# Expert rows in blocks of 256 and of 128 on one Trainium2 core, and another order of the work between the layers

## The reference, cut to what matters

```python
# layer 0: each token goes to its best expert alone
top1 = argmax(x @ gate_W + gate_b)
h = gelu(x[top1 == e] @ W1[e] + b1[e])          # 128 -> 512
out[top1 == e] = h @ W2[e] + b2[e]              # 512 -> 128
x = x + attention0(xn) * silu(out)
# layer 1: each token goes to its two best experts, each of which keeps at most C = 2048 rows
xe[idx1, pos1], xe[idx2, pos2] = x, x           # rows in order of arrival
h = gelu(xe[e] @ W1[e] + b1[e]);  ye = h @ W2[e] + b2[e]
out = w1 * keep1 * ye[idx1, pos1] + w2 * keep2 * ye[idx2, pos2]
x = x + attention1(xn) * silu(out)
```

## Time and profile before

| | us |
|---|---|
| median of 3 runs (lowest, highest) | 1130.6 (1126.27, 1135.07) |
| the profiled execution, its own time | 1132.19 |
| span of its profile | 1130.3 |
| PE busy in the span | 1004.9 (89%) |
| mean granted TensorE clock | 0.951 of full speed |

### The profile page before, as it was taken

One profiled execution on the slowest core, in us unless ns is written; L12 is line 12 of the kernel. 1 busy time (PEld: TensorE's weight loads), 2 busy tenths in 40 slices (PEclk: granted clock), 3 DMA queues, 4 the chain that ended last, 5 costly groups with the idle time before them and its releaser, 6 DMA issues.

```text
span 1130.3 us, 22358 instructions
## 1 busy us (share of the span) xinstructions
PE 1004.9 (89%) x6636; PEld 736.4 (65%) x6636; DVE 686.6 (61%) x2541; ACT 655.2 (58%) x1967; POOL 673.2 (60%) x825
## 2 busy tenths in 40 slices
PE   6688899999999999899999998998889979999940
PEld 2465566666668986566666665666568758989940
DVE  6847776776753346776786777868654443445326
ACT  4329767667754557667666766675554434454534
POOL 5534588888754555676675687887354423545533
PEclk9759899999999999999999999999999889999985
DMA  9200202202526742303302212132130044777755
GB/s 300 58 6 1 43 25 61 65 25 66 160 47 209 221 129 63 74 6 70 65 7 60 54 36 61 34 67 53 40 86 19 29 144 144 214 216 217 214 139 142
DMA packets 97385, 103.70 MB, mean 92 GB/s; under 512 B 10447, under 2 KB 85238, under 8 KB 97040
## 3 DMA queue, kind: packets, MB, share of 16 engines
q1 hardware_dynamic: 90256, 89.96, 30.5%
q0 software_dynamic: 7040, 12.66, 3.3%
HBM read 77.29 MB, written 25.28 MB: 91 GB/s over the span
## 4 chain that ended last, share of the span: by engine, by line
PE 62%; DVE 17%; ACT 7%; issue 6%; POOL 4%; DMA 1%; another core or an unknown queue 1%; SPq 0%; POOLq 0%; DVEq 0%; ACTq 0%
PE bank L1135 11%; PE bank L644 9%; PE bank L633 9%; PE bank L1164 7%; PE bank L1191 5%; PE bank L1179 4%; PE bank L1216 4%; DVE arena L1760 4%; PE bank L1154 3%; ACT arena L1494 3%; DVE arena L1769 2%; POOL arena L910 2%; PE bank L1365 2%; PE bank L1349 1%; ACT arena L1483 1%
## 5 line engine op out<-in xcount | busy, mean ns | idle before, releaser
L1494 ACT ACTIVATE arena<-arena 128x128 f32<-128x128 f32 (+1 forms) x512 | 226.9, 446 | 114.6 <-DVE arena L1760 114.0
L1760 DVE CUSTOM_DVE_ANT_0 arena<-bank,arena 128x128 f32<-128x128 f32 (+1 forms) x512 | 183.0, 413 | 140.8 <-PE bank L1164 133.1
L1135 PE MATMUL bank<-arena 128*128 128x512 f32 x384 | 215.6, 649 | 13.0 <-ACT arena L1483 10.0
L910 POOL TENSOR_TENSOR arena<-arena 128x512 f32<-128x512 f32 x128 | 133.5, 1046 | 146.6 <-ACT arena L1470 141.7
L1769 DVE COPY arena<-bank 128x384 f32<-128x384 f32 x256 | 130.2, 549 | 24.5 <-PE bank L1179 21.4
L607 POOL DMA_INDIRECT expert_out<-arena x78 | 77.0, 988 | 100.8 <-DVE arena L713 85.1
L1470 ACT ACTIVATE arena<-bank 128x512 f32<-128x512 f32 x192 | 112.4, 586 | 31.1 <-PE bank L1135 30.9
L925 POOL TENSOR_TENSOR arena<-arena 128x512 f32<-128x512 f32 x128 | 129.5, 1045 | 1.3
L1164 PE MATMUL bank<-arena 64*128 64x128 f32 (+1 forms) x1024 | 120.8, 355 | 9.6 <-DVE arena L1760 8.9
L1179 PEld LDWEIGHTS bank<-const,arena 128*128 128x128 f32 x768 | 91.9, 142 | 56.8 <-issue 56.6
L1191 PE MATMUL bank<-arena 128*64 128x256 f32 (+1 forms) x1024 | 112.3, 340 | 7.3 <-DVE arena L1769 3.7
(11 more groups left out here) (273 smaller groups left out, 1740.5 us busy)
## 6 DMA issues: line engine op xcount, KB each, us to landing
arena<-in_wp SPq DMA_DIRECT2D x39, 514.0 KB
arena<-recip_rows SPq DMA_DIRECT2D x30, 512.0 KB
XN<-in_wp SPq DMA_DIRECT2D x23, 514.0 KB
arena<-expert_rows SPq DMA_DIRECT2D x62, 129.0 KB
arena<-expert_out SPq DMA_DIRECT2D x16, 256.0 KB, 5.0
arena<-in_b SPq DMA_DIRECT2D x62, 64.0 KB
expert_out<-fill SPq DMA_DIRECT2D x11, 338.6 KB, 8.2
expert_rows<-fill SPq DMA_DIRECT2D x1, 2967.0 KB, 22.0
```

The lines of the kernel that those rows point to most:

```text
L910: pool.tensor_tensor(sq[:, i % 2], r, r, ALU.mult).then_inc(S["sq_done"], 1)
L1135: mm = pe.matmul(RING[bnk][:, :], xa[:, p, t * P:(t + 1) * P], wqkv[:, 512 * k:512 * k + 512], start=True, stop=True)
L1494: ins = act.activation(w, w, ACT.Exp, bias=nm[:, p, 16 * t + h:16 * t + h + 1], scale=-1.0, accum_out=den[:, p, 16 * t + h:16 * t + h + 1])
L1760: ins = v.tensor_tensor_reduce(out=SPb[:, c % 2, 384 * k + P * t:384 * k + P * t + n], in0=SBANK[k][:, P * t:P * t + n], in1=alibi[:, h, N ...
```

## The change

- A unit is 128 rows (BLK = 128). The units that always suffice are (4096 + 8*127) // 128 = 39 in layer 0 and (8192 + 8*127) // 128 = 71 in layer 1. They are worked through as blocks of two units and nine blocks of one: 15 + 9 = 24 blocks in layer 0, 31 + 9 = 40 in layer 1. `SMALL` lists the single ones: in layer 0 blocks 5, 7, ... 19 (every other one) and 23, in layer 1 every fourth, 7, 11, ... 39. For a single block all of its work is halved (rows loaded, turn, up, gelu, down, add_b2, one send), except for its weights, which are loaded whole.
- The tables grow: for each expert its pairs of units and what is left; the `owner` and the start row of every block, in both layers. In layer 0 `blocks` stays in step 0, `owners` moves to step 1 and `tables` is new there; SP now reads the start row by a register load in layer 0 too. In layer 1 `owners` and `tables` stand together after rows_max1(11).
- Parts that loop (four blocks in the body) are cut to where the pattern of single blocks repeats (`PERIOD`); the rest is written out.
- Behind the loop the scores have two banks, and PE makes scores(b+2) at the end of step1(b); DVE takes rows_max1 two sequences ahead of residual, with the mask and table work between them. `project` of sequence 15, `turn_last`, `logits_last` and `ranks1` stand elsewhere among the steps, and all of `project` goes through one bank. POOL does scale_out(15) before its scatters. SP fills the padding (now 128 rows a strip) before it loads the first weights.
- `fold_weights` moves from ahead of step 7 into step 6.

```diff
-BLK = 256
+
+
+
+BLK = 128
+DBL = 2 * BLK
 CAP = 2 * 2 * T // E
-NBLK0 = (T + E * (BLK - 1)) // BLK
-NBLK1 = (2 * T + E * (BLK - 1)) // BLK
-
-
-
-SPAN, CENTRE = 2 * T + BLK, T
+UNITS_OF = ((T + E * (BLK - 1)) // BLK, (2 * T + E * (BLK - 1)) // BLK)
+NSMALL = E + 1
+NBIG = tuple((u - NSMALL) // 2 for u in UNITS_OF)
+NBLK0, NBLK1 = (n + NSMALL for n in NBIG)
+
+SMALL = ((5, 7, 9, 11, 13, 15, 17, 19, 23), tuple(range(7, 40, 4)))
+SMALL_OF_FOUR = ((1, 3), (3,))
+PERIOD = ((4, 19), (4, 39))
...
+        def blocks(v, link, layer, held, nthr):
+
+
+            FX, UX, CGX, HALF, UNI, _, _, CMP, _ = TAB[layer]
+            cm = CMP[:, 0:E * nthr].rearrange("p (e k) -> p e k", e=E)
+            half = HALF.rearrange("p (e k) -> p e k", k=2)
+            v.memset(FX[:, 0:1], 0.0)
+            v.memset(UX[:, 0:1], 0.0)
+            link(v.scalar_tensor_tensor(out=cm, in0=held.unsqueeze(2).to_broadcast([P, E, nthr]), scalar=1.0 / BLK,
+                                        in1=cc(C_JJ, nthr).unsqueeze(1).to_broadcast([P, E, nthr]), op0=ALU.mult, op1=ALU.is_gt))
+            link(v.tensor_reduce(half, cm.rearrange("p e (k two) -> p e two k", two=2), AX.X, ALU.add))
+            v.tensor_tensor_scan(FX[:, 1:E + 1], ones[:, 0:E], half[:, :, 1], 0.0, ALU.mult, ALU.add)
+            link(v.tensor_tensor(UNI, half[:, :, 0], half[:, :, 1], ALU.add))
+            v.tensor_scalar(FX[:, 1:E + 1], FX[:, 1:E + 1], float(NBIG[layer]), None, ALU.min)
+            link(v.tensor_tensor_scan(UX[:, 1:E + 1], ones[:, 0:E], UNI, 0.0, ALU.mult, ALU.add))
+            link(v.scalar_tensor_tensor(out=CGX, in0=FX, scalar=-2.0, in1=UX, op0=ALU.mult, op1=ALU.add))
...
+        def owners(v, link, layer):
...
+            link(ins)
+            link(v.tensor_reduce(RSJ[0:1, 0:n], cj, AX.X, ALU.add))
+            v.tensor_scalar(owner[:, 0:n], RSJ[0:1, 0:n], -1.0, float(E - 1), ALU.add, ALU.min).then_inc(S["owner_ready"], 1)
...
+        def tables(v, link, layer):
...
+            link(v.tensor_tensor(steps[:, :, 0:E], first[:, :, 1:E + 1], first[:, :, 0:E], ALU.subtract))
+            for k, (lo, hi) in enumerate(((0, nb), (nb, n))):
+                ins = v.tensor_tensor(cj[:, lo:hi], cj[:, lo:hi], steps[0:1, k].unsqueeze(1).to_broadcast([1, hi - lo, E + 1]), ALU.mult)
+            link(ins)
+            link(v.tensor_reduce(RSJ[0:1, 0:n], cj, AX.X, ALU.add))
+            for lo, hi, size in ((0, nb, DBL), (nb, n, BLK)):
+                ins = v.scalar_tensor_tensor(out=RSJ[0:1, lo:hi], in0=const[0:1, C_JJ:C_JJ + hi - lo], scalar=float(size),
+                                             in1=RSJ[0:1, lo:hi], op0=ALU.mult, op1=ALU.add)
+            link(ins)
+            v.tensor_scalar(rowtab[layer][:, 0:n], RSJ[0:1, 0:n], float((NOROWS0, NOROWS)[layer]), None, ALU.min)\
+             .then_inc(S["tables_ready"], 1)
...
+        def single(layer, j, q):
+            return j in SMALL[layer] if isinstance(j, int) else q in SMALL_OF_FOUR[layer]
...
-            def load_rows(j, q):
-                row = sp.value_load(rowtab[0:1, bass.ds(j, 1)], min_val=0, max_val=NOROWS) if layer else j * BLK
-                src = xe[layer][bass.ds(row, BLK), :].rearrange("(t p) d -> p t d", p=P)
-                sp.dma_start(xb[:, q], src).then_inc(S[f"rows_in{q}"], 16)
-
-            def load_weights(j, q):
-
-                e = sp.value_load(owner[0:1, bass.ds(j, 1)], min_val=0, max_val=E - 1)
+            def load_rows(j, q, i):
+                n = 1 if single(layer, j, q) else 2
+                row = sp.value_load(rowtab[layer][0:1, bass.ds(entry(layer, j, q, i), 1)], min_val=0, max_val=(NOROWS0, NOROWS)[layer])
+                src = xe[layer][bass.ds(row, n * BLK), :].rearrange("(t p) d -> p t d", p=P)
+                sp.dma_start(xb[:, q, 0:n], src).then_inc(S[f"rows_in{q}"], 16)
...
-            sp.wait_ge(S["owner_ready"], layer + 1)
+                load_weights(j + NBUF, q, i + 1)
+
             if layer:
-                sp.wait_ge(S["ttr_done"], NB * 16)
-                for j in range(NBUF):
-                    load_weights(j, j)
-                sp.wait_ge(S["tables_ready"], 1)
+                sp.wait_ge(S["pads_ready"], 1)
                 for e in range(E):
                     row = sp.value_load(padtab[0:1, e:e + 1], min_val=0, max_val=NOROWS)
-                    sp.dma_start(xe[1][bass.ds(row, BLK), :].rearrange("(p r) d -> p (r d)", p=P), fill[:, :]).then_inc(S["filled"], 16)
+                    sp.dma_start(xe[1][bass.ds(row, BLK), :], fill[:, 0:ROW]).then_inc(S["filled"], 16)
+                sp.wait_ge(S["ttr_done"], NB * 16)
+                sp.wait_ge(S["owner_ready"], 2)
+                for j in range(NBUF):
+                    load_weights(j, j, 0)
+                sp.wait_ge(S["tables_ready"], 2)
...
-                for t in range(2):
+                for t in range(1 if single(layer, j, q) else 2):
...
                 pe.wait_ge(S[f"w_in{q}"], (i + (counts[q] + 1)) * 32)
+                n = BLK if single(layer, j, q) else DBL
                 for c in range(FC):
-                    mm = pe.matmul(HB[2 * (q % 2) + c // 2][:, (c % 2) * BLK:(c % 2 + 1) * BLK],
-                                   wb[:, q, c * P:(c + 1) * P], xbT[:, q % 2, :], start=True, stop=True)
+                    mm = pe.matmul(HB[2 * (q % 2) + c // 2][:, (c % 2) * DBL:(c % 2) * DBL + n],
+                                   wb[:, q, c * P:(c + 1) * P], xbT[:, q % 2, 0:n], start=True, stop=True)
...
             norm_root(len(SETS) - 2)
+            scale_out(NB - 1, 1)
+            last_ids()
             send_rows(2, 1)
-            last_ids()
-            scale_out(NB - 1, 1)
             send_rows(3, 0)
             for k in range(2):
                 residual0(len(SETS) - 1, k)
             norm_root(len(SETS) - 1)
+            send_rows(3, 1)
             send_rows(4, 0)
-            send_rows(3, 1)
             send_rows(4, 1)
             send_rows(5, 0)
...
                 pe.wait_ge(S["z1_evac"], b + 1)
-                pe.matmul(SC[:, 0:P], z1[:, p, 0:P], x[:, 0:P], start=True, stop=True)
-                pe.matmul(SC[:, P:P + N], z1[:, p, P:N], x, start=True, stop=True).then_inc(S["s1_full"], 1)
+                if b >= 2:
+                    pe.wait_ge(S["ttr1_done"], b - 1)
+                pe.matmul(SC[p][:, 0:P], z1[:, p, 0:P], x[:, 0:P], start=True, stop=True)
+                pe.matmul(SC[p][:, P:P + N], z1[:, p, P:N], x, start=True, stop=True).then_inc(S["s1_full"], 1)
 
             def weigh1(b):
                 pe.wait_ge(S["v1_evac"], b + 1)
@@ -1369,9 +1465,6 @@
             def step1(b):
 
                 p = b % 2
-                if b + 1 < NB:
-                    pe.wait_ge(S["ttr1_done"], b + 1)
-                    scores1(b + 1)
                 pe.wait_ge(S["exp1_done"], b + 1)
                 if b:
                     pe.wait_ge(S["pt1_evac"], b)
@@ -1382,6 +1475,8 @@
                     zv1(b + 2)
                 if b:
                     weigh1(b - 1)
+                if b + 2 < NB:
+                    scores1(b + 2)
 
             def turn_last(m):
 
@@ -1401,31 +1496,32 @@
             logits_last(8)
             zv1(1)
             scores1(0)
+            scores1(1)
             step1(0)
-            ranks1(3, MISC)
+            pe.wait_ge(S["lg_evac"], 1)
+            ranks1(3, RT)
+            for half in range(2):
+                project(NB - 1, 1, 0, half)
             step1(1)
-            pe.wait_ge(S["lg_evac"], 1)
+            for half in range(2):
+                project(NB - 1, 1, 1, half)
+            pe.wait_ge(S["rank_evac"], 5)
             turn_last(9)
-            pe.wait_ge(S["rank_evac"], 5)
-            project(NB - 1, 1, 0, 0)
-            project(NB - 1, 1, 1, 0, Y2)
             step1(2)
             logits_last(9)
-            project(NB - 1, 1, 0, 1)
-            project(NB - 1, 1, 1, 1, Y2)
             step1(3)
             step1(4)
+            pe.wait_ge(S["lg_evac"], 2)
+            turn_last(10)
             pe.wait_ge(S["y_evac"], 2 * NB)
             ranks1(4, MISC)
             step1(5)
-            pe.wait_ge(S["lg_evac"], 2)
-            turn_last(10)
+            logits_last(10)
             step1(6)
-            logits_last(10)
             step1(7)
-            step1(8)
             pe.wait_ge(S["rank_evac"], 6)
             ranks1(5, MISC)
...
                         counts(v, link, mem0)
                     if routing and c == 4:
-                        blocks(v, link, CNT0[:, 0:8], CNT0[:, 8:16], CNT0[:, 16:24], CNT0[:, 24:32], CMP0)
-                    if routing and c == 5:
-                        owners(v, link, 0, CNT0[:, 16:24], CMP0, mem0[1][0:1, 0:NJ])
+                        blocks(v, link, 0, CNT0[:, 0:8], T // BLK)
+                    if late and c == 2:
+                        owners(v, link, 0)
+                    if late and c == 3:
+                        tables(v, link, 0)
...
             rows_max1(0)
             for k in range(2, 5):
```

(52 more changed lines are left out.)

229 lines of the change are left out of this document (137 added, 92 removed).

## The result

The changed kernel takes **1125.6 us** (median, 1115.9 to 1129.2) beside 1130.5 (1126.3 to 1135.1) of the kernel before. The ratio is 0.9947 with an interval from 0.9931 to 0.9963, so it is faster by some 5 us, where I had forecast 22. The profiled execution has a span of 1125.8 us against 1130.3.

A forecast was written before the change was run, and what follows sets the result against it. PE's work was taken as the bound, with sends limiting the smaller blocks. Savings of 3.4 (layer 0's experts), 5.9 (layer 1's) and 12.8 us (behind the loop) sum to 22.1, giving a median of 1108.5 us, range 1094 to 1126.

The forecast's parts named there:

- the term "4 us": Behind the loop: 4 us left in the stretch for a VectorE wait of 5.80 us with no named cause.
- the term 1 us for the tables in step 1: Step 1: owners and tables, some 5 us in two portions beside idle time of VectorE, cost 1 us.
- Steps 0 and 1: Before layer 0's experts: owners leaving step 0 offsets added blocks and tables work; sum 0, from -2 to +3 us.
- Behind the loop: Last loop turn to layer 1's experts: fewer PE waits and slow-clock matmuls; 12.8 us saved, bounds 6 to 18.8.
- lower bound of 6: Behind the loop: least saving, 6 us, with the full 5.8 us unnamed wait twice and its slow clock.
- Layer 0's experts: 13.0 us less PE work, 9.6 us returned as waits for sends: 3.4 us saved, bounds 0.2 to 5.8.
- The ring: Experts: VectorE's add, send, landing and next evac_x form a cycle; 6.8 us per pair in layer 0, not 5.60.
- rival 4: Layer 0's experts: PE's waits lower the granted clock, pairs take 11.2 us; slower than before at 1142 us; chance 0.04.
- Layer 1's experts: 13.0 us less PE work, 7.2 us returned as waits for sends: 5.9 us saved, bounds 1 to 10.6.
- The sum of PE's work: Both layers' experts: a single block taken as half a whole one, 1.87 against 3.73 us; 13.0 us less each.
- rival 2: Experts: each block costs the same whatever its size, +7.5 us, with -12.8 behind the loop: 1125 us; chance 0.10.
- Rival 3: Behind the loop: nothing gained, waits only move to the tables and the unnamed wait: 1121 us; chance 0.14.

The follow-up runs named there:

- call 1: First group of runs, all on one chip: the changed kernel unaltered and three variants, beside the kernel before at a median of 1126.6 us.
- no_silu: Changed kernel without the SiLU of layer 0's experts, so each send starts about 1.7 us sooner; ratio 0.9835 to the kernel before.
- const_rows: Changed kernel with layer 0's row addresses worked out from block numbers, not loaded from a table by SyncE; ratio 0.9872 to the kernel before.
- order_only: Kernel before, blocks of 256 kept, with only the new order behind the loop; ratio 0.9911 to the kernel before.
- calls 2, 3 and 5: Three later groups of runs, each on another chip, beside the kernel before at medians of 1112.6, 1112.3 and 1113.1 us.

## Why the prediction was wrong

The forecast was 22.1 us off the profiled execution, and 4.5 came. Of the 17.6 that are missing, 7.9 are missing behind the loop, 7.2 in the loop itself, and 2.7 in the two layers' experts. The step that failed first is the term "4 us" for the wait that the profile doesn't name; it is a family of waits beside GpSimd's scatters, also in the loop, where the sum had nothing. The next is the term 1 us for the tables in step 1, which cost 6 in every profile and are hidden in the table by a step 0 that happened to be short.

- **Steps 0 and 1 (0, from -2 to +3): failed.** "Each beside some 2 us in which DVE idles, so 1 us stays" is the step of it. VectorE's idle time is spread over the step; 2.5 us of owners and 7.0 of tables in two pieces outrun it. PE waited for 4.1 us, and the granted clock was 0.82 for the 10 us behind the wait. Step 1 takes 45.9 to 47.5 us in every profile with the tables in one piece, 39.9 to 40.1 without them and 40.1 to 40.7 with them spread. I had also priced the operations at 0.2 to 0.5 us each, and five of the nine of `tables` take 0.9 to 1.3 there. Step 0 does get shorter (it ends at 122.4 in the mean of 16 profiles against 126.7 of 4), but single executions spread by 10 us.
- **Behind the loop (-12.8, measured -4.9): right in its parts, one term mis-sized.** Waits ahead of the ranks gone, tables hidden, fills out of the way: as said. The "wait ended by nothing that the profile names", which I gave 4 us, is not one wait but a family of them in the runs of scatters. At the level of call 1, that of the profiles shown, they and the slow clock behind them cost 8.5 to 12.6 us (78.4 without the scatters, 86.9 to 91.0 with them). At the other level the stretch is 82.2 to 83.0 with the order alone or the whole change, where the forecast was 82.6 by the same bounds. Its gain is even so 8.3 there and not 12.8, since the kernel before has fewer stalls there too (91.3 and not 95.4). The measured 4.9 also lie below the lower bound of 6, and that bound was added up wrongly: 5.8 twice in place of 4 leaves 5.2 of the 12.8, before any slow clock.
- **The loop (0, not named): missed.** The same stalls sit in its runs of scatters: the step before the last takes 40.1 to 44.1 us at one level and 35.5 to 36.4 at the other, with either kernel. Beyond them the profiled execution had the late landing of `recip_rows`. Over all profiles the loop is no longer with the change (422.1 us in the mean of seven against 421.7 of two at the upper level, 414.4 of nine against 414.2 of two at the lower), so the +7.2 is an accident of the two executions in the main. The late landing is not wholly one: it came in ten of sixteen profiles with small blocks in layer 0 and in none of four without.
- **Layer 0's experts (-3.4): the mechanism right in part, two terms mis-sized.** The ring is in the way (`no_silu`), SyncE's register load is not (`const_rows`), but a pair takes 7.3 us and not 6.8, and PE's work fell by 8.8 us and not 13.0. -2.0 in the profile; over all profiles -2.2 at one level, +1.7 at the other. Of rival 4, the clock, a little came: in the experts of layer 0 it was 1.00 in this profile but 0.95 to 0.96 in seven of the sixteen with small blocks, 0.98 to 1.00 in the four without.
- **Layer 1's experts (-5.9): the size held, with luck.** -4.6 in the profile, 3.9 to 5.8 at this level and 4.9 to 7.6 at the other against the one profile there of the kernel before (`order_only`, with the same blocks, has 1.6 less than that). But PE's work fell by 9.8 us and not 13.0, its idle time grew by 5.1 and not 7.2, and of its waits 5.7 us are for rows and 2.1 for the ring that the prediction named.
- **The sum of PE's work (13.0 in each layer).** It took a single block as half a whole one. The busy times say 8.8 and 9.8. Whether the smaller matmuls are slower or short waits are counted as busy, no run tells.
- **The rivals.** The measured time is that of rival 2 (1125), by luck in the main: it had layer 1's experts 3.7 us longer and they are 4.6 shorter, and of its 12.8 behind the loop 4.9 came. For layer 0 it was nearly right in effect, since a pair of a whole and a single block takes 7.3 us where two whole ones were 7.46 of PE's work. Rival 3 (1121, the waits moved to the tables and the unnamed wait) was right on the unnamed wait and wrong on the tables. The outcome, faster by under 1%, had 0.21 of the chances.
- **The whole.** At the level without the stalls the changed kernel has 0.9888 (12 us by the ratio, 9 by the medians), and with the tables spread 0.9862, some 15.

## What to carry to other kernels

Before calling a moved piece of work hidden, compare its length as one piece with the idle time of its engine at that very place; cut in four, a table of 7 us on VectorE cost PE 0.2 us in place of 6.1, and became 4.2 us long itself. Price small operations from rows beside the same neighbour engine, not from a quiet stretch. When matmuls are halved, don't take half of their time for granted: PE's busy time fell by 8.8 and 9.8 us where the halves promised 13. A wait that the profile doesn't name isn't a constant to be carried over: look at what every other engine does while it lasts, and take that away once.

## What the runs showed of the hardware

- **Runs of GpSimd's indirect scatters hold the other engines back, in some calls.** Idle times of 2 to 9 us on VectorE, ScalarE and PE with no named cause lie inside or just behind runs of four to twelve scatters; 28 scatters replaced by computation took all of them behind the loop away (87 to 91 us became 78.4). In calls 2, 3 and 5 the same runs of eight had none on VectorE and ScalarE. Each call had another chip; whether the chip or something else makes the difference, the runs don't tell.
- **A packet of instructions can delay a small write.** One of 16,384 bytes takes about 1 us, and a write of 16 KB whose last packets stood behind it landed after 3.1 to 3.6 us in place of 1.4, in ten of twenty profiles.
- **VectorE's small operations wait for GpSimd's.** At 136 to 143 us GpSimd has tensor operations of 1.04 to 1.32 us back to back, and VectorE's take 0.99 (128 x 8), 1.13 (128 x 16), twice 1.3 (1 x 135 and 1 x 81) and 0.90 (1 x 24), each ending within 0.2 us of the end of one of GpSimd's. Behind the loop, with GpSimd idle, L480 takes 0.18 on 128 x 16, the two of L482 (1 x 279 and 1 x 81) 0.59 together, and L489 0.17, as the rows below show. The Trainium skill, SBUF — State Buffer, section SBUF: two separate sides, calls the port pair that the two engines share an exclusive lock: an operation of VectorE with two inputs in SBUF waits for the whole of one of GpSimd's that reads SBUF, and so does one in what the Trainium skill calls a 2-port perf mode. The trace agrees for L480 and L482, which have two inputs. The two others, L478 and L489, have one, and whether they ran in such a mode the trace doesn't show. By that rule tables belong where GpSimd doesn't compute.

```profile
914.18 0.18 DVE L480 TENSOR_TENSOR arena<-arena 128x16 f32<-128x16 f32 x1
914.39 0.59 DVE L482 TENSOR_TENSOR arena<-arena 1x279 f32<-1x279 f32 x2
...
915.86 0.17 DVE L489 TENSOR_SCALAR arena<-arena 1x40 int32<-1x40 f32 x1
```
